# A token tower on one core: copies, score products and row statistics moved inside the full turns

## The reference

```
h = table[ids]
x = layernorm(h)
# mixer, on rms(x): proj = rms(x) @ in_proj.T -> zgate, u (512 wide), B, C (16), dt (8 heads)
u, B, C = silu(conv4([u, B, C]));  B, C normed;  d = softplus(dt)
for t in tokens:                       # linear recurrence per head
    z = (z + d*(u*B - A*y)) / (1 + d*d*A);  y = y + d*z
    out[t] = y @ C[t]
x = x + ((out + D*u) * silu(zgate)) @ out_proj.T + b
# MLP
x = x + gelu(rms(x) @ fc1.T + b1) @ fc2.T + b2
h = h + x
h = h + int8_linear(layernorm(h))      # one scale over all rows: max|layernorm(h)|
```

## Time and profile before

| | us |
|---|---|
| median of 3 runs | 1282.46 (1280.84 to 1283.85) |
| the profiled execution's own time | 1284.41 |
| its span in the trace | 1282.6 |
| TensorE busy in the span | 1156.4 (90%) |
| VectorE busy | 1104.9 (86%) |
| ScalarE busy | 786.7 (61%) |
| GpSimd busy | 715.7 (56%) |

### The profile page before, as it was taken

How to read it: one execution, slowest core, us unless ns; L and a number is a source line. 1 busy time by engine, 2 the same in 40 slices (tenths; PEclk the granted TensorE clock), 3 DMA queues, 4 the chain that set the end, 5 groups by cost and what they waited for, 6 DMA issues and landing times. The chain is left out here.

```text
span 1282.6 us, 25093 instructions
## 1 busy us (share of the span) xinstructions
PE 1156.4 (90%) x7328; PEld 766.2 (60%) x7328; DVE 1104.9 (86%) x1988; ACT 786.7 (61%) x1275; POOL 715.7 (56%) x2062
## 2 busy tenths in 40 slices
PE   2893078999999999999999999999999999999987
PEld 1551033667576767666666767576767676757554
DVE  5999979879898989898989999898989897876188
ACT  4666747374847484848475666657574748462358
POOL 8882010748585858585858585857576666740000
PEclk9999999899999999999999999999999999998999
DMA  9999921010101010101010000000010101000015
GB/s 355 408 407 417 420 71 38 1 36 1 37 1 37 2 36 2 33 5 30 9 26 14 21 18 17 18 17 19 16 27 9 35 0 36 2 19 1 1 66 196
DMA packets 38034, 93.17 MB, mean 73 GB/s; under 512 B 10270, under 2 KB 21875, under 8 KB 33635
## 3 DMA queue, kind: packets, MB, share of 16 engines
q1 hardware_dynamic: 34338, 82.89, 18.3%
q0 software_dynamic: 3072, 8.39, 1.7%
q10 hardware_dynamic: 576, 1.31, 0.3%
HBM read 82.86 MB, written 9.70 MB: 72 GB/s over the span
## 5 line engine op out<-in xcount | busy, mean ns | idle before, releaser
L826 POOL TENSOR_TENSOR stp<-Gs,X 128x32 f32<-128x32 f32 x900 | 260.9, 290 | 254.8 <-ACT X L799 172.7
L828 POOL TENSOR_TENSOR Gs<-Gs,stp 128x32 f32<-128x32 f32 x900 | 274.6, 305 | 70.4
L1270 PE MATMUL bank<-w_fc,gl 128*128 128x256 f32 x1024 | 243.0, 383 | 0.1
L1251 PE MATMUL bank<-mT,w_fc 128*128 128x512 f32 x512 | 236.7, 596 | 1.8 <-ACT mT L1231 1.7
L1270 PEld LDWEIGHTS bank<-w_fc,gl 128*128 128x128 f32 x1024 | 191.8, 191 | 54.3 <-issue 25.8
L659 PE MATMUL bank<-xT,w_in 128*128 128x512 f32 x448 | 205.5, 600 | 8.7 <-DVE uT L1159 8.7
L990 ACT ACTIVATE uT<-bank,cols 128x512 f32<-128x512 f32 x60 | 45.0, 775 | 221.1 <-DVE sz L1166 162.6
L1251 PEld LDWEIGHTS bank<-mT,w_fc 128*128 128x128 f32 x512 | 94.9, 190 | 85.9 <-issue 79.9
L659 PEld LDWEIGHTS bank<-xT,w_in 128*128 128x128 f32 x448 | 81.4, 190 | 92.3 <-issue 78.1
L1004 DVE SCALAR_TENSOR_TENSOR uT<-bank,cols,uT 128x508 f32<-128x508 f32 (+1 forms) x180 | 125.0, 733 | 2.1
L369 DVE TENSOR_TENSOR peak<-ring,peak 128x1536 f32<-128x1536 f32 (+2 forms) x67 | 115.4, 1722 | 12.9 <-ACT ring L268 10.7
(11 more groups left out here) (230 smaller groups left out, 1961.0 us busy)
## 6 DMA issues: line engine op xcount, KB each, us to landing
ring<-in_table SPq DMA_DIRECT2D x31, 1536.0 KB, 20.6
d_rep<-d_rows SPq DMA_DIRECT2D x128, 64.0 KB, 2.0
out<-res SPq DMA_DIRECT2D x14, 512.0 KB, 2.9
b_rep<-bc_rows SPq DMA_DIRECT2D x128, 32.0 KB, 1.8
c_rep<-bc_rows SPq DMA_DIRECT2D x128, 32.0 KB, 1.8
w_fc<-in_w_fc SPq DMA_DIRECT2D x2, 1024.0 KB, 14.6
ring<-in_table SPq DMA_DIRECT2D x2, 768.0 KB, 12.1
w_in<-in_w_in ACTq DMA_DIRECT2D x1, 1088.0 KB, 5.1
```

What stands on the lines that cost most here:

```text
L826: pool.tensor_tensor(stp[:], Gs[:, t, ::-1, :], X2[:, t, :, :], ALU.mult).then_inc(rec.sem, 1)
L828: pool.tensor_tensor(Gs[:, t + 1, :, :], Gs[:, t, :, :], stp[:], ALU.add).then_inc(rec.sem, 1)
L1251: last = pe.matmul(pj[n % 4][:, :], w_fc1[:, k, n * P:(n + 1) * P], mT[:, k, :], start=(k == 0), stop=(k == KD - 1))
L1270: last = pe.matmul(sbk[j // 2][:, (j % 2) * D:(j % 2 + 1) * D], gl[n % LEAD][:, j * LEN:(j + 1) * LEN], w_fc2[:, n, :], start=False, stop= ...
```

## The change

Four edits, all for full turns. The row statistics of group g + 1 go from ahead of the first masks to behind them. `act_utok` can be called for a part of the sequences: copies 0 and 1 go behind gelu 5 (the sixth), ahead of the layer norm, and copies 2 and 3 stay behind gelu 7 (the eighth). Transposes 2 and 3 go from n = 9 to n = 7, between fc1(7) and fc2(4). The first scores go from n = 10 to n = 8, ahead of fc2(5). Turn 1 and the turns behind the loop keep their order.

```diff
-        def act_utok(act, g):
-            act.wait_ge(kq.sem, kq.at(g))
-            if since(g):
-                act.wait_ge(y_mm.sem, y_mm.at(g - 1))
-            for j in range(G):
+        def act_utok(act, g, seqs=range(G)):
+            if 0 in seqs:
+                act.wait_ge(kq.sem, kq.at(g))
+                if since(g):
+                    act.wait_ge(y_mm.sem, y_mm.at(g - 1))
+            for j in seqs:
                 act.wait_ge(u_T.sem, u_T.at(g, j + 1))
                 act.activation(utok[:, j, :], tb[j % 2][:, :], ACT.Copy).then_inc(utok_ready.sem, 1)
...
-                    if second and first and n == FT + 1:
-                        if not third:
-                            pe_warm(pe, sbk[0], 1)
+                    if second and first and third and n == FT - 1:
+                        pe_u_T(pe, p, g, 2)
+                        pe_u_T(pe, p, g, 3)
+                    if second and first and third and n == FT:
+                        pe_scores(pe, p, 0)
+                    if second and first and not third and n == FT + 1:
+                        pe_warm(pe, sbk[0], 1)
                         pe_u_T(pe, p, g if first else None, 2)
                         pe_u_T(pe, p, g if first else None, 3)
-                    if second and first and n == FT + 2:
+                    if second and first and not third and n == FT + 2:
                         pe_scores(pe, p, 0)
-                        if not third:
-                            pe_warm(pe, sbk[0], 4)
+                        pe_warm(pe, sbk[0], 4)
                     if third and n >= LEAD:
                         pe_fc2(pe, m, n - LEAD)
...
+                    if second and first and n == 5:
+                        act_utok(act, p, (0, 1))
                     if second and n == 5:
                         act_layer_norm(act, p)
                 if second and first:
-                    act_utok(act, p)
+                    act_utok(act, p, (2, 3))
...
-                if nxt and not filling:
+                if nxt and not second:
                     dve_row_stats(dve, g + 1)
...
                 if nxt and filling:
                     dve_quantise(dve, g + 1)
+                if nxt and second and not filling:
+                    dve_row_stats(dve, g + 1)
                 if first and third:
                     dve_h2(dve, m)
```

## The result

| | us |
|---|---|
| kernel before, median of 4 runs | 1281.65 (1280.71 to 1283.85) |
| changed kernel, median of 4 runs | 1332.32 (1330.52 to 1333.66) |
| ratio | 1.0391, 95% interval 1.0379 to 1.0404 |
| predicted | 1320 (1300 to 1344), slower 0.95 |

The change costs 50.7 us (1332.32 - 1281.65). The profiled execution has a span of 1331.9 us and a mean granted clock of 0.971, against 1282.6 us and 0.993 before.

A forecast was written before the change was run, and what follows sets the result against it. The prediction took TensorE, busy 59.44 of 60 us, to bound the kernel. From the median, 1282.5 + 22.8 (net wait over fourteen turns) + 15 (clock falls) = 1320 us, range 1300 to 1344.

The forecast's parts named there:

- TensorE's gaps alone count: In full turns only TensorE's own gaps can shorten a turn: 0.55 us a turn, some 7 us in all.
- Transposes sooner, at no cost: Transposes 2 and 3 between fc1(7) and fc2(4) wait for nothing; their 0.88 us is only moved.
- The wait at the scores: TensorE waits in front of the first scores for gelu seven and two copies: 1.9 us a turn, 1.8 to 2.0.
- Masks sooner bring nothing here: First masks on VectorE come sooner, but the first scan product was not waiting for them: counted 0, at most 0.2 us.
- Statistics at no cost, but 2.4 us a turn if their cover is gone: Row statistics behind the first masks hide there; uncovered, they cost 2.4 us only when VectorE bounds the second masks.
- Net per turn of 1.63 us: Per full turn, 1.9 us at the scores less 0.27 at the second `pe_u`; 22.8 us over fourteen turns.
- The clock: Clock falls behind the new wait at the scores in 5 of 14 turns: 15 us, possible 0 to 42.
- The second rival: Clock falls in nearly every full turn, 9 to 14, at 3.0 us each: 1341 us; chance 13%.
- the case that the prediction held likeliest: The forecast itself: clock falls in 1 to 8 full turns, 1308 to 1330 us; chance 53%.
- two comparable waits: TensorE waits in the earlier trace: 1.52 us behind the loop with a clock fall, 1.23 us at 248.04 without.
- The first rival: The wait at the scores is paid but the clock never falls: 1282.5 + 22.8 = 1305 us; chance 27%.

The follow-up runs named there:

- bias edit: Kernel before with the fc2 bias on VectorE (1.2 us) behind the skip of tiles 2 and 3 instead of ahead of it: 1273.66 us, ratio 0.9936.
- copies first: Changed kernel with copies 2 and 3 ahead of gelu 7 on ScalarE instead of behind it: 1291.27 us, ratio 1.0073.
- wait filled: Changed kernel with two 512-column matmuls that nothing reads, on TensorE ahead of the first scores in full turns: 1306.65 us, ratio 1.0194.

## Why the prediction was right, step by step

- *TensorE's gaps alone count*: right, and shown by the bias edit: 0.55 us a turn was nearly all there was (the list of waits has one more, 0.2 us once in twelve turns), and it could be had.
- *Transposes sooner, at no cost*: right. They wait for nothing, and the copies start at 617.29.
- *The wait at the scores*: right. Forecast 1.8 to 2.0 us, measured 1.86 to 1.98 in the full turns. Its makers were gelu seven and two copies, as the run with copies first shows.
- *Masks sooner bring nothing here*: right; VectorE waits for TensorE in front of both sets.
- *Statistics at no cost, but 2.4 us a turn if their cover is gone*: right in this change. Without the cover TensorE waits 1.95 us a turn more, not 2.4, and the clock falls on top, which this step did not count.
- *Net per turn of 1.63 us*: right. 1.71 in the run with the wait filled, where the wait at the second `pe_u` shrinks from 0.55 to 0.22 us; 25 us in all against 22.8.
- *The clock*: this term was too small, 15 us against 25.7, and that is most of the 12 between 1320 and 1332; some 2 more lie in the wait. The term had two factors, and both were off. I expected falls in 5 of 14 turns at 3.0 us each; there were 13. But most were short: a turn with a fall takes 65.27 us (65.22 to 65.38) in nine cases and 66.8 to 67.05 in four, against 63.73 with the clock up, so the nine cost 1.5 us each, and the four 3.3. The single fall in the kernel before was a long one. The reason for going below half, the dense fc2 part ahead of the wait, did not protect the clock. The second rival, with 13%, had the count right, and its price per fall was too high: 1341. That the errors of the two factors go opposite ways, so that 1332 lies between the two sums, is in part luck: the case that the prediction held likeliest, falls in 1 to 8 turns, did not come. Its two comparable waits were too few to count from. The wait of 1.52 us behind the loop stands, unchanged to 0.01 us, in all twelve profiled kernels, and the clock falls behind it in six of them (half of these times long, half short) and in six it does not. One of the six without a fall is the kernel before with the statistics moved:

```profile
1211.67 2.01 PE L1131 MATMUL bank<-Qf,Kf 32*128 32x64 f32 x64 [1.52 <-ACT gl L1261]
```

```profile
1211.00:1220.00 9.00, 8.33 (x171) 7.52 (x172) 5.22 (x8) 2.49 (x5) 0.00 (x0) 1.00 0.01 4
```

- *The first rival* (the clock holds) gave 1305. That is the time with the gap filled (1306.65), and 27 us under the time with it open. The rule of the Trainium skill (TensorE: Matmul & The Clock Gate, section Why this matters for your kernels), by which gaps this short are harmless, gave the same sum. This trace does not agree with it: the clock fell at 13 of 14 gaps of 1.86 to 1.98 us.

## What to carry to other kernels

Where one engine is busy 99% of a stage, moving work sooner on it can win no more than its gaps, so look at what each moved instruction waits for and what is queued behind it; here two copies stood behind an activation that itself waited. The kernel's one real gap was closed by moving 1.2 us of work on another engine behind the operation that TensorE wanted. In this kernel an idle gap of 2 us on TensorE cost about twice its length: once as time, and once more through the clock.

## What the runs showed of the hardware

- A single idle gap of 1.9 to 2.0 us in each turn of some 65 us, with TensorE otherwise dense, brought the clock from 2.4 to 1.2 GHz in 13 of 14 turns. A gap of 0.85 to 1.04 us did so in 2, one of 0.14 to 0.27 us in none. A gap of 2.5 us at another place in the turn did so in 13.
- The gap's length does not decide alone: one of 1.52 us at a place that no edit touched was followed by a fall in six of twelve profiled kernels, and one of 1.86 us in the changed kernel by none. What else decides was not tried.
- Matmuls whose result nobody reads, put into the gap, kept the clock up and bought 25.7 us, without the scores coming any sooner within the turn.
- The same 120 operations of a recurrence on GpSimd were busy 35.2 us in one kernel and 37.6 in another, with one constant different between the two, the step of the recurrence behind which GpSimd makes the norm factors.
